# Attention inside a two-layer kernel: the scores for the maxima run three pairs of heads ahead instead of four

## The reference

```
q, k, v = split_heads(x @ Wq), split_heads(x @ Wk), split_heads(x @ Wv)
attn = einsum('bhqd,bhkd->bhqk', q, k) * scale
attn = softmax(attn, axis=-1)
attn = attn + bias[None]                # from rel_table
out = einsum('bhqk,bhkd->bhqd', attn, v)
```

## Time and profile before

| | us |
|---|---|
| median of 3 runs (lowest to highest) | 2348.91 (2347.59 to 2349.43) |
| the profiled execution's own time | 2351.22 |
| its span, first to last instruction | 2349.5 |
| attention stage, about | 990 to 1434 |
| one group in the middle of it | 12.40 |

### The profile page before, as it was taken

One profiled execution on the slowest core, in us unless ns is written; L12 is line 12 of the kernel. 1 busy time (PEld: TensorE's weight loads), 2 busy tenths in 40 slices (PEclk: granted clock), 3 DMA queues, 4 the chain that ended last, 5 costly groups with the idle time before them and its releaser, 6 DMA issues. The chain is left out here.

```text
span 2349.5 us, 30894 instructions
## 1 busy us (share of the span) xinstructions
PE 1818.1 (77%) x8636; PEld 1079.1 (46%) x8637; DVE 1363.7 (58%) x2196; ACT 946.4 (40%) x1725; POOL 613.8 (26%) x594
## 2 busy tenths in 40 slices
PE   5888885814997398689999993244599999999990
PEld 2333332813665254334444431243466666666660
DVE  7999983765111522288888850979544444444436
ACT  6777774400332231057777771110033333333330
POOL 0000000021443000001111112220166666666653
PEclk9999997555999599869999985556899999999995
DMA  3000002540110963343333414454333433333318
GB/s 112 0 0 1 0 36 80 174 143 14 60 59 19 315 237 118 93 74 92 88 85 87 87 47 156 163 189 155 125 58 65 64 64 62 61 62 62 60 16 286
DMA packets 164482, 215.53 MB, mean 92 GB/s; under 512 B 30355, under 2 KB 119838, under 8 KB 164128
## 3 DMA queue, kind: packets, MB, share of 16 engines
q1 hardware_dynamic: 122784, 141.23, 20.1%
q0 software_dynamic: 41600, 73.08, 14.0%
HBM read 136.90 MB, written 83.23 MB: 94 GB/s over the span
## 5 line engine op out<-in xcount | busy, mean ns | idle before, releaser
L1195 PE MATMUL f_h_ps<-W,f_XT 128*128 x736 | 351.5, 600 | 1.1 <-ACT f_XT L1246 1.1
L1210 PE MATMUL f_y_ps<-W,f_HT 128*128 x1472 | 348.9, 380 | 1.7 <-DVE f_HT L1299 1.7
L1767 DVE TENSOR_REDUCE att_MX<-att_s_ps 128x2 f32<-128x1024 f32 x256 | 305.1, 1221 | 65.8 <-PE att_s_ps L1646 63.5
L1162 POOL DMA_INDIRECT moe<-f_Y,TOK x184 | 268.9, 1461 | 272.8 <-ACT f_Y L1266 256.5
L1749 ACT ACTIVATE att_PT<-att_st_ps 128x512 f32<-128x512 f32 x512 | 278.3, 597 | 97.3 <-PE att_st_ps L1671 86.4
L1210 PEld LDWEIGHTS f_y_ps<-W,f_HT 128*128 128x128 f32 x1472 | 266.0, 191 | 31.7 <-issue 3.1
L303 PE MATMUL rec_gate<-rec_XC,rec_W 128*128 128x512 f32 x384 | 187.9, 643 | 67.4 <-ACT rec_R L205 42.8
L1671 PE MATMUL att_st_ps<-att_Q,att_K 50*128 50x512 f32 x512 | 223.0, 500 | 19.7 <-ACT att_PT L1749 17.2
L1299 DVE COPY f_HT<-f_ht_ps 128x512 f32<-128x512 f32 x184 | 125.9, 684 | 150.9 <-PE f_ht_ps L1203 148.0
L1646 PE MATMUL att_s_ps<-att_K,att_Q 48*128 48x512 f32 x512 | 192.4, 478 | 25.6 <-DMA att_K<-qk_pairs 20.7
L1153 POOL DMA_INDIRECT f_XG<-x,TOK x184 | 192.1, 1044 | 57.2 <-issue 55.5
(11 more groups left out here) (207 smaller groups left out, 2631.4 us busy)
## 6 DMA issues: line engine op xcount, KB each, us to landing
W<-in_w POOLq DMA_DIRECT2D x48, 512.0 KB, 12.1
x<-n_Y SPq DMA_DIRECT2D x24, 512.0 KB, 4.9
n_X<-x SPq DMA_DIRECT2D x24, 512.0 KB, 8.8
n_Y<-moe SPq DMA_DIRECT2D x24, 512.0 KB, 8.8
att_Q<-qk_pairs SPq DMA_DIRECT2D x192, 64.0 KB, 2.9
att_K<-qk_pairs SPq DMA_DIRECT2D x192, 64.0 KB, 3.0
qk_pairs<-prj_HI SPq DMA_DIRECT2D x16, 512.0 KB, 3.3
qk_pairs<-prj_LO SPq DMA_DIRECT2D x16, 512.0 KB, 5.4
```

The source lines that it names most:

```text
L1162: nc.gpsimd.indirect_dma_start(out=outs[n % len(outs)], out_offset=bass.IndirectOffsetOnAxis(ap=TOK[:, n:n + 1], axis=0), in_=Y[n % R][:], ...
L1195: mm = nc.tensor.matmul(h_ps[r % 2][:], XT[r % 2][:, c], W1[:, bass.ds(e * W_EXPERT + c * F, F)], start=(c == 0), stop=(c == DC - 1))
L1210: mm = nc.tensor.matmul(y_ps[r % 2][:], HT[r % 2][:, f], W2[:, bass.ds(e * W_EXPERT + f * D, D)], start=(f == 0), stop=(f == FC - 1))
L1767: nc.vector.tensor_reduce(MX[n % 2][:, qc, :, p], s_ps[m % 2][:], AX.X, ALU.max).then_inc(s_mx, 1)
```

## The change

`LEAD` goes from 4 to 3: pair i + 3's scores are computed in pair i's slots. A group's maxima are then complete after p = 0, so `split` moves to the end of p = 0 on DVE, the maxima's transposes move from the second slot of p = 0 to the first slot of p = 1 on PE, and `copy_maxima` on ACT moves from the second slot of p = 0 to the second slot of p = 1. The thresholds of the two waits that guard `x_ps` are moved by one group to fit. `scale(n - 2)` stays after the first maximum of p = 1.

```diff
-LEAD = 4
+LEAD = 3
...
                 pe.wait_ge(s_ms, n + 1)
                 if n >= 1:
                     pe.wait_ge(s_mh, n)
-                if n >= 4:
-                    pe.wait_ge(s_tmp, n - 3)
+                if n >= 3:
+                    pe.wait_ge(s_tmp, n - 2)
...
             def sums_T(n):
                 pe.wait_ge(s_ot, n + 1)
-                pe.wait_ge(s_mh, min(n + 4, NGROUPS))
+                pe.wait_ge(s_mh, min(n + 3, NGROUPS))
...
-                    if p == 0 and slot == 1 and n + 1 < NGROUPS:
+                    if p == 1 and slot == 0 and n + 1 < NGROUPS:
                         maxima(n + 1)
...
-                    if p == 0 and kc == 1 and n + 1 < NGROUPS:
+                    if p == 1 and kc == 1 and n + 1 < NGROUPS:
                         copy_maxima(n + 1)
...
-                if p == 1 and i + LEAD < TWO:
+                if p == 0 and i + LEAD < TWO:
                     split((i + LEAD) // 2)
```

## The result

The changed kernel takes 2445.71 us (median of 5 runs, 2444.14 to 2449.55) against 2348.91 us beside it: ratio 1.0417, 95% interval 1.0403 to 1.0432. It is 97 us slower. The forecast was 2405, in a range of 2390 to 2465. Of the 97 us about half is the wait and the late copy that were forecast, and about half a fall of TensorE's clock that was not. The profiled execution took 2444.8 us, its span is 2443.0 us, its mean granted clock 0.838.

A forecast was written before the change was run, and what follows sets the result against it. PE was taken as nearest to the bound, DVE and ACT close. Groups 2 to 29 add 28 x 2.0 = +56, groups 0 and 1 +1.2, group 30 -1.5: together +56 on 2351.2, 2407, by the median 2405; range 2390 to 2465.

The forecast's parts named there:

- Lead-in: Before the loop: three pairs of scores instead of four, gain 0, since the first group's maxima DMA releases the loop.
- The wait in b0: First slot of a group's second pair of heads: PE's transposes wait 1.6 us for DVE's scale.
- The wake-up: From DVE's end of the scale to PE's transposes: taken as 0.2 us, bounds 0.1 and 0.35.
- Program order on PE: b1's scores (next slot) cannot pass the waiting transposes, so the whole wait is paid and DVE and ACT run dry.
- The late copy: ACT's maxima copy after b1: second DMA issues at 12.54 us, lands 1.8 later, next group starts at 14.4.
- PE's own path: Group length by PE's slots and ACT's copy, without the DMA: 14.0 to 14.3 us, DMA last by little.
- The group at the full clock: Attention groups 2 to 29: each goes from 12.40 to 14.4 us, 28 x 2.0 = +56.
- The clock: PE's granted clock in the middle of attention: expected to stay 1.00 from 1040 to about 1450.
- The rival: Clock falls in attention: half level for a fifth of each group, +52, 2457 us; chance 0.15.
- The end of the stage: Group 30: first half keeps scores and full clock, second half loses a little: -1.5 us.
- The landing collides: Rival: maxima copies land beside SP's loads, 2.9 us instead of 1.8, +31, 2436 us; chance 0.15.
- The wait takes the place of other waits: Rival: the stall absorbs PE's existing waits, group 12.3 us, kernel 2340 or 2345 us; chance 0.07.

The follow-up runs named there:

- Run 1: Changed kernel with DVE's scale(n-2) put ahead of the first maximum of p = 1 instead of behind it: 2368.1 us, ratio 1.0059 to 1.0123.
- run 3: Kernel before, LEAD = 4 kept, with only the later maxima's transposes, later copy and two thresholds of the change: 2437.3 us.
- run 4: Changed kernel with ACT's copy of the maxima one slot earlier, after the first slot of p = 1: 2420.1 us.
- run 2: Changed kernel with 8 extra score matmuls a group in PE's wait for the scale: 2420.8 us.
- run 9: Changed kernel with the maxima's copy one slot earlier and 8 extra score matmuls in PE's wait for the scale: 2391.4 us.
- run 10: Changed kernel with 4 extra score matmuls a group in PE's wait for the scale: 2408.9 us.

## Why the prediction was right, and where it was not

- **Lead-in: right.** The loop starts at 1016.6, again released by the maxima's landing, now after 5.92 us of idle where it was 2.35. No gain.
- **The wait in b0: right to 0.06 us.** Forecast 1.6 us with the transposes 8.96 us into the group; measured 1.54 and 8.93. The wake-up taken as 0.2 was 0.15; the lower bound was 0.1. Run 1 shows the cause, run 3 that it is not the lead.
- **Program order on PE: right.** All of the wait is paid (b1's scores start at 1184.04, behind the transposes), and DVE and ACT run dry behind it (1.44 and 2.27 us of idle). This is what the Trainium skill (TensorE: Matmul & The Clock Gate, Part 2) says of matmuls, and the trace agrees.
- **The late copy: right in kind, a little off in size.** Second DMA issue forecast at 12.54, measured 12.37 (1186.40 + 0.55 - 1174.58). Landing 1.8, as taken; the 2.0 us of the Trainium skill (DMA: Bandwidth & Descriptors, Anatomy of one DMA) are slightly more than these transfers took, and less than the 2.9 us (median) that the earlier trace rows show beside SP's loads. Group start 14.25 instead of 14.4. PE's own path was 14.03 (14.25 less the 0.22 us of idle), inside the 14.0 to 14.3 forecast, so the DMA was last by little, as said. The 13.80 of run 4 is lower because its edit also takes ACT's copy out of that path.
- **The group at the full clock: right.** 14.25 against 14.4; 28 groups give +52 against +56.
- **The clock: wrong.** The forecast kept PEclk at 1.00 in the middle and gave its fall a chance of 0.15. It was 0.83, and cost 48 us, half of the loss. This is the step that failed, and a PEclk below 1 in the middle was one of the prediction's own signs of being wrong. The rival had its price nearly right (+52), but partly by luck: it took the half level for a fifth of each group, and it was a third of the time. What I had in hand was one fall after 0.73 us of idle with two slots without scores, and I weighed the scores that go on more than the longer wait. Runs 2, 9 and 10 show that the wait itself brings the clock down: filled with extra work, in groups of the same length, it does so far less.
- **The end of the stage: right in kind, too small.** Forecast -1.5 us for group 30; measured -8.1 from group 30 to the last transposes. The clock stayed up not only through the first half, where the scores go on, but also through the second.
- **The landing collides: did not happen.** Median 1.8 us, 2.3 at most.
- **The wait takes the place of other waits: did not happen.** A group never came near 12.4.

Two slips in the working change nothing of this. The 1.53 us "of waits" in a group before are a difference of starts; PE idles only 0.58 us there by its own row (11.82 busy of 12.40). And 28 x 1.9 is 53, not 52; 28 x 1.8 = +50 alone gives 2399, and the lower bound of 2390 is reached only if the lead-in's and the end's gains are taken off too.

So the sign and the mechanism of the wait were right, and the likeliest time was 41 us too low, because the cost of a wait on PE was counted once. The clock's 48 us were partly made up by 4 us less in the groups at full clock and 7 us more gained at the end. The measured 2446 is above 2442, the upper bound by the sum's own terms; it is inside the range only because the range was widened for the rivals.

What stays open: which groups fall to the half level, how much of the second 48 us each of the two waits brought, and why half of the filling (run 10) did no less than all of it (run 2).

## What to carry to other kernels

When a shared buffer's reader and writer are moved next to each other, look at what stands ahead of the reader on its own engine: here one reduction ahead of the scale cost 1.54 us a group, and two moved lines gave it back. On PE, count a new wait twice, once as time and once as the slower matmuls that may follow; a version that fills the wait with needless work tells the two apart. Put small work of PE into the idle that is already there (the end of a0), not where it closes a chain.

## What the runs showed of the hardware that I had not expected

- A wait of 1.54 us once in 14.25 us, with PE busy for most of the rest, went with a granted clock that spent a third of the time at the half level (0.83); with 0.41 us of it left idle and the copy early (run 9) it was 0.99. In run 1 two short idles, 0.21 and 0.51 us, one slot apart, came ahead of a fall; they stand in every group of that run, and 24 of 28 groups had no fall. The Trainium skill (TensorE: Matmul & The Clock Gate, Why this matters for your kernels) ties the fall to longer idle gaps than any of these; these runs do not agree.
- Needless matmuls made a kernel faster: 2420 to 2391 us (run 4 to run 9), and 2446 to 2421 and 2409 (runs 2 and 10).
